# A graph network kernel on one core: the one-hot of a gathered group's nodes made by ScalarE from distances

## What is computed

```python
for l in range(5):
    h = leaky(x @ W1[l] + b1[l]) @ W2[l] + b2[l]                 # each node, hidden width 128
    e = leaky(edge_attr @ We1[l] + be1[l]) @ We2[l] + be2[l]     # each edge
    msg = h[src] * e * dot_scale[l]
    agg = segment_sum(msg, dst)                                  # onto the destination nodes
    out = x + agg * res_w[l]
    x = layernorm(out) * ln_g[l] + ln_b[l]
```

## Time and profile before

| | |
|---|---|
| time, median of 3 runs | 6694.78 us (6693.1 to 6714.96) |
| time of the profiled execution | 6661.36 us |
| its span, first to last instruction | 6659.3 us |
| mean granted TensorE clock, of full speed | 0.896 |
| setup, up to the first edge step | some 1260 us |
| busy: PE, DVE, POOL, ACT | 84%, 77%, 68%, 18% of the span |

### The profile page before, as it was taken

The page is one execution under the profiler, slowest core; times in us unless marked ns, Lnnn a source line. Parts: engine busy times, 40 slices in busy tenths (PEclk is TensorE's granted clock), DMA queues, the critical chain, the costliest instruction groups (busy, mean ns, idle before and its releaser), DMA issues.

```text
span 6659.3 us, 172226 instructions
## 1 busy us (share of the span) xinstructions
PE 5572.3 (84%) x64844; PEld 3690.2 (55%) x64845; DVE 5150.9 (77%) x7991; ACT 1205.6 (18%) x1852; POOL 4528.9 (68%) x4793
## 2 busy tenths in 40 slices
PE   6776788788888888888878888888888887888887
PEld 2223444456666555666655666665566665556665
DVE  8997533588887678888758887867888775888886
ACT  0000332211122211112221111221111222111111
POOL 5777777566667467777727777755777773777775
PEclk9998666899999889999979999988999997999997
DMA  3112488755556445556635555644556563566664
GB/s 134 26 26 48 107 212 208 189 133 140 139 140 159 107 117 134 146 142 149 160 75 135 141 147 144 154 126 103 129 144 147 147 161 80 138 147 152 151 174 111
DMA packets 733557, 886.39 MB, mean 133 GB/s; under 512 B 325488, under 2 KB 502976, under 8 KB 731568
## 3 DMA queue, kind: packets, MB, share of 16 engines
q1 hardware_dynamic: 568480, 703.64, 40.2%
q0 software_dynamic: 152144, 154.93, 11.7%
q10 hardware_dynamic: 12096, 16.53, 0.8%
HBM read 749.51 MB, written 125.06 MB: 131 GB/s over the span
## 4 chain that ended last, share of the span: by engine, by line
PE 44%; issue 18%; DVE 16%; POOL 13%; DVEq 4%; ACT 3%; DMA 1%; ACTq 0%; SPq 0%; POOLq 0%
PE bank L977 14%; POOL slots L775 12%; PE bank L973 8%; PE bank L1026 7%; PE bank L1051 5%; PE bank L1013 3%; DVE arena L1662 3%; DVEq L1782 2%; DVE arena L1750 2%; ACT arena L1241 2%; DVE arena L1670 2%; DVE x_packed L1670 2%; PE bank L855 2%; PE bank L840 2%; DVE nodes_state L1718 2%
## 5 line engine op out<-in xcount | busy, mean ns | idle before, releaser
L788 POOL DMA_INDIRECT arena<-h_rows,src x3855 | 3675.2, 953 | 1703.1 <-issue 1258.5
L977 PEld LDWEIGHTS bank<-w2s,arena 128*128 128x128 f32 x8960 | 1182.7, 212 | 772.5 <-DVE arena L1750 437.6
L977 PE MATMUL bank<-w2s,arena 128*128 128x128 f32 x8960 | 1314.6, 304 | 211.0 <-DVE arena L1750 193.2
L775 POOL DMA_INDIRECT slots<-arena,slot_index x792 | 788.0, 995 | 267.4 <-issue 241.5
L973 PE MATMUL bank<-nodes_state,edge_w 64*128 64x512 f32 x980 | 593.8, 688 | 307.4 <-DVE nodes_state L1718 143.0
L1051 PEld LDWEIGHTS bank<-arena 112*64 112x64 f32 x20160 | 640.4, 138 | 268.3 <-issue 247.1
L1051 PE MATMUL bank<-arena 112*64 112x64 f32 x20160 | 725.9, 225 | 61.5 <-issue 55.6
L1241 ACT ACTIVATE arena<-bank,tenth 128x512 f32<-128x512 f32 x490 | 335.5, 685 | 2305.7 <-PE bank L973 2305.7
L973 PE MATMUL bank<-x_packed,edge_w 64*128 64x512 f32 x1260 | 735.9, 665 | 16.9 <-ACT std L1188 16.0
L1662 DVE SCALAR_TENSOR_TENSOR arena<-bank,edge_w,arena 128x512 f32<-128x512 f32 x490 | 366.9, 749 | 420.5 <-ACT arena L1241 414.6
L1670 DVE TENSOR_TENSOR x_packed<-bank,slot_rel 128x2880 f32<-128x2880 f32 (+8 forms) x315 | 589.3, 1871 | 15.8 <-issue 15.8
(11 more groups left out here) (198 smaller groups left out, 5632.3 us busy)
## 6 DMA issues: line engine op xcount, KB each, us to landing
arena<-slot_pick SPq DMA_DIRECT2D x630, 448.0 KB
arena<-h_rows SPq DMA_DIRECT2D x630, 224.0 KB
x_packed<-slot_attr SPq DMA_DIRECT2D x630, 128.0 KB
nodes_state<-attr_t SPq DMA_DIRECT2D x485, 128.0 KB
arena<-h_rows,src POOLq DMA_INDIRECT x3855
slot_pick<-arena SPq DMA_DIRECT2D x126, 448.0 KB
slots<-arena SPq DMA_DIRECT2D x9, 1904.0 KB, 22.2
arena<-slots SPq DMA_DIRECT2D x126, 136.0 KB
```

What stands on the lines that cost most here:

```text
L775: pool.indirect_dma_start(slots, bass.IndirectOffsetOnAxis(ap=slot_index[:, t:t + 1], axis=0), records[:, v, j, :], None).then_inc(record_ ...
L788: pool.indirect_dma_start(to[0:n, at:at + D], None, table, bass.IndirectOffsetOnAxis(ap=index[0:n, t:t + 1], axis=0)).then_inc(landed(t), 16)
L977: mm = pe.matmul(to[:, j * P:(j + 1) * P], acts[:, j * TILE:(j + 1) * TILE], w2s[:, :], start=True, stop=True)
```

## The change

Only the making of `pick` moves. DVE no longer makes it. ACT makes it, behind the middle part of its step, from the distance of each column number to the edge's node: the absolute value of `rel` minus the column number, and then one minus it, kept at zero or more. This is one at distance zero and zero at every other whole distance. The absolute value takes one instruction for each of the 8 tiles, since the bias is one number for each partition; the second takes one instruction on 128x640, in place, and first waits for the last of the 8. Column numbers are copied once into a new buffer on chip. Before it writes a `pick` buffer ACT waits until the group that used it last has been summed, and PE waits for the new `pick` before `window_sums`.

```diff
         src = sb("src", [P, RING_SLOTS, TPG], I32)
+        window_column = sb("window_column", [P, WIN])
...
+        pick_begun, pick_ready = sem("pick_begun"), sem("pick_ready")
...
                 def window_sums(k):
+                    pe.wait_ge(pick_ready, l * GR + real(k) + 1)
                     for j in range(TPH):
...
+                def window_pick(m):
+                    r = l * GR + real(m)
+                    if real(m) > 1:
+                        act.wait_ge(win_ready, 2 * (r - 1))
+                    for t in range(TPG):
+                        at = real(m) * TPG + t
+                        ins = act.activation(pick[:, m % 2, t, :], window_column[:, :], ACT.Abs, scale=-1.0,
+                                             bias=rel[:, at:at + 1])
+                    ins.then_inc(pick_begun, 1)
+                    act.wait_ge(pick_begun, r + 1)
+                    act.activation(pick[:, m % 2, :, :], pick[:, m % 2, :, :], ACT.Relu, scale=-1.0, bias=ones[:, 0:1]
+                                   ).then_inc(pick_ready, 1)
+
                 def step(s, part):
...
                     part("middle")
+                    m = a_at(s + 1)
+                    if m is not None and m != SPILL_AT:
+                        window_pick(m)
...
             prepared(dve.tensor_copy(column, column_i))
+            prepared(dve.tensor_copy(window_column[:, :], column[:, 0:WIN]))
...
                     m, i = a_at(s + 1), b_at(s + 1)
-                    if m is not None and m != SPILL_AT:
-                        at = real(m) * TPG
-                        one_hot(pick[:, m % 2, :, :], TPG, WIN, rel[:, at:at + TPG])
```

## The result

The changed kernel takes 6722.86 us (median of 20 runs, 6691.96 to 6741.29), the kernel before 6694.51 us (20 runs, 6657.87 to 6714.96). The ratio is 1.0042, 95% interval 1.0028 to 1.0057: 28 us slower, with 19 to 38 us inside the interval. It is in the range of the prediction (6665 to 6738), 25 us above its point and a little beyond the 0.3% that it called no change. The profiled execution has a span of 6704.7 us, against 6659.3.

A forecast was written before the change was run, and what follows sets the result against it. PE was busiest (84%, 44% of the chain of waits), DVE on the path only in part. Terms -25 + 23 + 5 + 0.3 = +3 us, put on the 6694.8 median, gave 6698 us; range 6665 to 6738.

The forecast's parts named there:

- the relief: On DVE, 485 picks of 396.5 us leave; gain taken as 25 us, ends 22 and 37.
- DVE's wait for ACT: Sign at the leaky step: this wait grows from 414.6 us by over 200.
- the length: A pick on ACT lasts 3.1 us from first to last, between 2.8 and 3.9; ACT rises to 41% busy.
- PE's wait for `pick` in the loop: Pick made a step ahead, over 5 us before use; costs PE only the waiting instruction, covered by running L977.
- the ends of the layers: Tails of the layers: 4.9 us each in four, about 3.5 in the last, 23 us slower in all.
- The four delays of a tail: In a layer's tail, late root and late sums in both slots: 1.0 + 1.3 + 1.0 + 1.6 = 4.9 us.
- one term: Loop slots, sub-step 4, 32 places: late tenth of B absorbed but for 0.15 us each, 5 us; ends 0 and 29.
- DVE's freed time: Faster rival: gains carry on as whole steps shorten, adding up to 123 us, 6600; chance 0.15.
- The table: Rival: absolute value in another table than the root, two loads per edge-step root, some 154 us, 6852; chance 0.03.
- The slower rival: ACT late at the 32 sub-steps and tails, deciding above about 3.3 us a pick; +68 us, 6763, at 3.9; chance 0.20.
- The rule that relu and the like belong on VectorE: Skill rule against the change: priced by engine time, 485 x 2.3 = 1115 us slower; no row supports such a price.

The follow-up runs named there:

- pick ahead: Changed kernel, but ScalarE makes the pick before the middle part of its step, not behind it; 6666.15 us, ratio 0.998 to the kernel before.
- no pick: Changed kernel with nobody making the pick and PE not waiting for it, one-hot of gathered groups left out; ratio 0.9979 to the kernel before.
- chunk sums first: Changed kernel, but in sub-step 5 of loop slots PE does chunk sums ahead of window sums; ratio 1.0009 to the kernel before.
- pick on both engines: Changed kernel with VectorE's one-hot kept beside it, into a buffer nobody reads; ratio 1.0093 to the kernel before.

## Why the prediction was right and wrong

**Right, the relief.** It put the gain between 22 and 37 us and took 25; the steps show 22.0. The 0.41 us a step came out as worked, but in 55 steps, not 80; the prediction's lower end, 22, had counted only what PE waits for. The runs without a pick put the relief lower, at 14 us (0 to 29), so 25 is not confirmed to better than that. DVE's wait for ACT grew by 210 us, where over 200 was said. DVE's busy time fell by 343.5 us and not by 396: neighbours overlap, and in the earlier trace rows the instruction behind the pick starts 0.73 us after it and not 0.82, which makes 485 x 0.73 = 354.

**Right, the length.** A pick was put at 3.1 us. It lasts 2.94 from first to last in the step shown, and keeps ACT for 2.64 us from the end of the biased half to the tenth, since neighbours overlap. ACT is busy 39%, not 41%. There is one table load, of 1283 ns, as in the kernel before; the Trainium skill, ScalarE: Activation LUTs, section Table sets, has abs in every set, and the trace agrees. PE's wait for `pick` in the loop costs nothing, as was said.

**Right in the sum, the ends of the layers.** 4.9 us each and 3.5 for the last were forecast, 23 in all; 4.6, 3.6, 4.3, 5.7 and 1.7 came, 19.9. The four delays of a tail, at the end of the third layer, PE in the changed kernel:

```profile
4498.72 2.04 PE L975 MATMUL bank<-nodes_state,edge_w 64*128 64x512 f32 x2 [1.90 <-ACT std L1191]
...
4513.98 1.34 PE L1016 MATMUL bank<-arena 128*64 128x80 f32 x16 [1.03 <-DVE arena L1682]
...
4535.86 2.05 PE L979 MATMUL bank<-w2s,arena 128*128 128x128 f32 x8 [1.80 <-ACT std L1191]
...
4547.06 1.33 PE L1016 MATMUL bank<-arena 128*64 128x80 f32 x16 [1.78 <-ACT arena L1266]
```

The first and the third are the late root: 0.7 us more than before, where 1.0 was forecast (the wait was 1.12 in the earlier trace rows). The last is the last group's sums, waiting for their pick, where nothing waited before; 0.3 us of it come back behind it, which leaves 1.5 for the forecast 1.6. The second has the size of the forecast 1.3 but another cause: not the pick, but DVE's leaky step, the same wait as in sub-step 5. Together they are 4.0 us a layer and 3.1 in the last, 19 in all. That single ends differ from this is the granted clock's doing in part. Just ahead of the third delay, where nothing waits for ACT yet, before and after:

```profile
4503.40 1.01 PE L827 MATMUL bank<-nodes_state,center 64*128 x2 [1.20 <-issue]
...
4528.10 1.85 PE L829 MATMUL bank<-nodes_state,center 64*128 x2 [1.23 <-issue]
```

The clock is at the upper level in the first and at 0.50 in the second, and so it is with the pick ahead too, where the delays are gone. This makes 1.6 us of the third layer's 4.3.

**Wrong, one term.** "It is absorbed, with 0.1 to 0.3 left here and there: 32 x 0.15 = 5 us." It is 29.5 + 2.8 = 32.3 us, above even the upper end of 29 and 27 us more than forecast, about the whole miss of 25. The step that failed is that the 32 places were priced from the one in the earlier trace rows. In that one only a B tenth follows the pick, and for those 12 the price was right: 0.3, 0.4 or 0, 2.8 us in all. In the other 20 an A tenth follows, and PE's window sums wait for its leaky step. That wait stands in the code one line ahead of the call, and the list of what PE waits for in a step, ahead of the prediction, leaves it out too; the prediction named DVE and the next hidden layer as those who wait for the late tenth, and not PE in the same step. With the 0.94 us of the step shown (0.79 in four of them) the 20 make some 18 us.

**Not foreseen, the clock.** The other 11 us come from four of the 20 places, which lose 2.57, 4.13, 4.18 and 4.21 us. The one of 4.21, in the third layer: the granted clock (PEclk, third from the end) of the same stretch before and after, then PE's matmuls after:

```profile
4378.10:4384.30 6.20, 5.41 (x106) 5.04 (x108) 4.27 (x9) 0.94 (x2) 4.68 (x6) 1.00 0.75 185
...
4399.70:4410.10 10.40, 10.40 (x106) 8.40 (x103) 3.62 (x9) 1.48 (x4) 7.69 (x9) 0.53 0.40 96
```
```profile
4399.14 1.32 PE L1016 MATMUL bank<-arena 128*64 128x80 f32 x16 [0.88 <-DVE arena L1682]
...
4401.43 3.25 PE L857 MATMUL bank<-node_w,y_act 128*112 128x64 f32 x16
```

The tile's h takes 3.25 us where the same 16 matmuls took 1.78 before: after PE's idle 0.88 us the clock goes to the lower level, 1.2 GHz, for some 10 us. In the kernel before it was at 2.4 GHz here, with no such wait. The two go together over all profiles near 6700 us. In the kernels without this wait (before, pick ahead, no pick, chunk sums first) the granted clock is 1.00 in each of the 20 steps; with it, it falls in 4 of 20 in the changed kernel and in 8 of 20 with the pick on both engines, in part in other steps. So in these steps the fall comes only with the wait, and the wait doesn't always bring it; what decides is not shown. The prediction had no term for it.

**The rivals.** DVE's freed time did not carry on: with no pick at all the kernel is at 0.9979 and not at 0.982. The table did not change. The slower rival had the right place, the sub-steps 4 and 5, and the wrong trigger: it was to decide above 3.3 us a pick, and picks are shorter. The loss was there at the length that the forecast took as harmless. The rule that relu and the like belong on VectorE (the Trainium skill, ScalarE: Activation LUTs, Rules for kernel authors) would have cost 1115 us by engine time, as the prediction worked out; the runs don't bear it out: with the pick ahead, the ACT version is no slower than DVE's (0.998).

## What to carry to other kernels

When work moves to an idle engine, its share of busy time says that it fits; its place in that engine's list says what it costs. Put it ahead of the instructions that wait anyway, not behind them and ahead of the next one that others need. When one delay repeats at many places, price one place of each kind: list who waits for the late result on every engine, in the same step too, above all waits that are there because two buffers share a bank.

## What was not expected of the hardware

An added idle of PE of 0.88 us, ahead of dense work, came with a fall of TensorE's granted clock to its lower level (0.53 over 10 us in the place shown). It did so in 4 of 20 like steps of one kernel and in 8 of 20 of another, and in none of 80 steps without that idle. Each fall costs 1.6 to 3.3 us, more than the wait. And on two chips each kernel, the one before too, took some 11200 us, with more than 1000 short waits of PE ahead of one line of matmuls where another chip had 57. There the kernels with the 4365 added instructions of ScalarE ran 0.5 to 0.8% longer than the kernel before, wherever the pick stood.
